# Two-layer graph transformer, 1024 nodes: a chunk of the output projection between the last two transpositions, and earlier spreading of the row sums

## The reference, cut

```python
for l in range(2):                       # the two attention rounds
    q = ((x @ Wq[l].T + bq[l]) * scaling).reshape(n, 8, 64)
    k = (x @ Wk[l].T).reshape(n, 8, 64)
    v = (x @ Wv[l].T).reshape(n, 8, 64)
    scores = jnp.einsum('ehd,ehd->eh', q[tgt], k[srcidx])     # one per edge and head
    w = softmax of scores over the edges of one target
    agg = segment_sum(w[:, :, None] * v[srcidx], tgt)
    attn = agg.reshape(n, 512) @ Wo[l].T + bo[l]
    x = batchnorm(x + attn, g1[l], beta1[l])
    x = batchnorm(x + relu(x @ W1[l].T + b1[l]) @ W2[l].T + b2[l], g2[l], beta2[l])
```

## Time and profile before

| | us |
|---|---|
| median of the runs shown | 1031.21 (1028.3 to 1032.97, 3 runs) |
| the profiled execution, device time | 1029.51 |
| its span, first to last instruction | 1027.7 |
| TensorE busy | 957.7 |
| VectorE, ScalarE, GpSimd busy | 625.0, 494.3, 251.2 |
| mean granted TensorE clock | 0.98 |

### The profile page before, as it was taken

The page is one execution under the profiler, slowest core; times in us unless marked ns, Lnnn a source line. Parts: engine busy times, 40 slices in busy tenths (PEclk is TensorE's granted clock), DMA queues, the critical chain, the costliest instruction groups (busy, mean ns, idle before and its releaser), DMA issues.

```text
span 1027.7 us, 15261 instructions
## 1 busy us (share of the span) xinstructions
PE 957.7 (93%) x5378; PEld 682.8 (66%) x5378; DVE 625.0 (61%) x1087; ACT 494.3 (48%) x767; POOL 251.2 (24%) x138
## 2 busy tenths in 40 slices
PE   6999999999998999999999999999999999999925
PEld 2835545888777886877777776746777776767313
DVE  4676476468777324437776675535576767636395
ACT  1665344555724213327666675213576666641054
POOL 2000000599932051410100047112100000660400
PEclk9999999999999999999999999999999999999967
DMA  9201100000200111146565673111076556712102
GB/s 328 73 0 41 41 1 21 1 1 1 83 1 1 50 73 41 62 143 184 169 189 180 186 223 103 41 41 42 21 210 188 177 164 186 235 52 66 39 1 82
DMA packets 58848, 96.14 MB, mean 94 GB/s; under 512 B 8284, under 2 KB 38172, under 8 KB 58270
## 3 DMA queue, kind: packets, MB, share of 16 engines
q1 hardware_dynamic: 55454, 93.11, 28.8%
q10 hardware_dynamic: 3328, 2.15, 0.7%
HBM read 59.58 MB, written 33.55 MB: 91 GB/s over the span
## 4 chain that ended last, share of the span: by engine, by line
PE 74%; POOL 7%; issue 6%; DVE 6%; ACT 4%; DMA 2%; SPq 0%; DVEq 0%; ACTq 0%; POOLq 0%
PE slots L1802 66%; PE slots L1869 9%; POOL MASK L702 3%; POOL MASK L696 1%; POOL KR L701 1%; DMA W<-in_wkT 1%; POOL X L733 1%; DMA PT<-blocks 1%; POOL PT L693 1%; ACT X L1118 1%; DVE X L1686 0%; POOL WL L713 0%; DVE SM L1663 0%; DVE st L1163 0%; ACT XTR L816 0%
## 5 line engine op out<-in xcount | busy, mean ns | idle before, releaser
L1802 PE MATMUL slots<-PT,XN 128*64 128x256 f32 x1024 | 117.6, 382 | 0.4 <-DMA PT<-blocks 0.2
L1591 DVE CUSTOM_DVE_ANT_0 SM<-slots,MASK 128x1024 f32<-128x1024 f32 x64 | 75.7, 1220 | 66.2 <-PE slots L1802 66.2
L1802 PE MATMUL slots<-KS,QS 64*128 64x512 f32 x768 | 105.7, 406 | 4.6 <-DVE nm L1591 3.5
L1802 PEld LDWEIGHTS slots<-PT,XN 128*64 128x64 f32 x1024 | 72.0, 137 | 42.8 <-issue 11.7
L758 POOL TENSOR_TENSOR QS<-QF,QS 128x512 fp32r<-128x512 f32 x16 | 20.7, 1291 | 320.4 <-ACT QS L1038 320.4
L1802 PEld LDWEIGHTS slots<-KS,QS 64*128 64x128 f32 x768 | 70.3, 184 | 25.1 <-issue 10.4
L805 ACT ACTIVATE PT<-slots 128x1024 f32<-128x1024 f32 x68 | 69.4, 1020 | 31.1 <-PE slots L1869 26.2
L1022 ACT ACTIVATE SM<-SM,nm 128x1024 f32<-128x1024 f32 x64 | 73.3, 1145 | 18.8 <-DVE nm L1591 18.1
L1022 ACT ACTIVATE PT<-PT,nm 128x1024 f32<-128x1024 f32 x64 | 73.3, 1145 | 16.9 <-DVE nm L1591 16.5
L1802 PE MATMUL slots<-PT 128*128 128x512 bf16 (+3 forms) x408 | 78.8, 364 | 2.3 <-ACT PT L805 1.2
L1591 DVE CUSTOM_DVE_ANT_0 PT<-slots,MASK 128x1024 f32<-128x1024 f32 x64 | 75.2, 1211 | 4.1 <-PE slots L1802 3.9
(11 more groups left out here) (403 smaller groups left out, 2163.1 us busy)
## 6 DMA issues: line engine op xcount, KB each, us to landing
blocks<-FL SPq DMA_DIRECT2D x56, 512.0 KB, 3.2
PT<-blocks SPq DMA_DIRECT2D x224, 128.0 KB, 3.4
X<-in_x SPq DMA_DIRECT2D x4, 512.0 KB, 11.9
W<-in_wout SPq DMA_DIRECT2D x2, 1024.0 KB, 6.2
W<-in_gq SPq DMA_DIRECT2D x2, 1024.0 KB, 5.1
W<-in_gk SPq DMA_DIRECT2D x2, 1024.0 KB, 5.1
spill<-X SPq DMA_DIRECT2D x4, 512.0 KB, 2.6
SXR<-XTR SPq DMA_DIRECT2D x1, 2048.0 KB, 8.4
```

What stands on the lines that cost most here:

```text
L1591: nc.vector.tensor_tensor_reduce(out=SMs[n % SMB], in0=src, in1=MASK[:, unit(n)[2], :], scale=-1.0, scalar=-0.1 * NO_EDGE, op0=ALU.add, op ...
L1802: return nc.tensor.matmul(o_, lhsT, rhs, start=start, stop=stop)
```

## The change

Two things. In `attention_order`, `rsum_bc` stands ahead of the pair of scores of its step and no longer behind it (0 to 2 in each round; `rsum_bc` 3 has no scores beside it). And in the tail, `wo` 0 is begun before `turn` 63: its chunk 0 stands between `turn` 62 and `turn` 63, chunks 1 and 2 right behind `turn` 63, ahead of `rsum` 3. For this the slots are given by a table: one slot is skipped at `rsum` 3 of each round, so that `wo` 0 has the slot of `turn` 61; `rsum` 3 has that of `agg` 14, `agg` 15 that of `turn` 62, `rsum_bc` 3 that of `turn` 63. All later jobs follow on, each four slots behind its forerunner as before. With the moved `rsum_bc`, six jobs around each take another forerunner: at the third one, for example, score 59 has the slot of score 56, not 57.

```diff
--- before.py
+++ after.py
@@ -68,10 +68,10 @@
         m = n - LAG
         if 0 <= m < UNITS:
             order += [("flip" if i in FLIPS_BEFORE else "turn", i) for i in (m, m + 1)]
+        if m >= 16 and m % 16 == 4 or m == UNITS + 2:
+            order.append(("rsum_bc", m // 16 - 1))
         if n < UNITS:
             order += [("score", n), ("score", n + 1)]
-        if m >= 16 and m % 16 == 4 or m == UNITS + 2:
-            order.append(("rsum_bc", m // 16 - 1))
         if n % 8 == 4 and 8 <= n < UNITS - 8:
             order.append(("q", n // 8 + 1))
         if n == 4:
@@ -173,6 +173,14 @@
 
 JOBS = job_table()
 INDEX = {name: j for j, (name, _) in enumerate(JOBS)}
+SLOT, SLOT_BEFORE, _last, _at = {}, {}, [None] * 4, 0
+for _name, _ in JOBS:
+    if _name[0] in ("rsum0g", "rsum1g") and _name[1] == H // 2 - 1:
+
+        _at += 1
+    SLOT[_name], SLOT_BEFORE[_name] = _at % 4, _last[_at % 4]
+    _last[_at % 4] = _name
+    _at += 1
 EVAC_COUNT = {}
 _seen = {"act": 0, "dve": 0, "dve_xT": 0}
 for _name, _engine in JOBS:
@@ -456,7 +464,7 @@
         shift_added, out_summed, nibbles_added, hid_cleared, w1_split, sum_ready = (
             sem(n) for n in ("shift_added", "out_summed", "nibbles_added", "hid_cleared", "w1_split", "sum_coefficients_ready"))
 
-        slot_of = lambda name, i: psum[:, INDEX[(name, i)] % 4, :]
+        slot_of = lambda name, i: psum[:, SLOT[(name, i)], :]
 
         def evacuated(name, i):
             engine = JOBS[INDEX[(name, i)]][1]
@@ -1789,9 +1797,8 @@
 
             def begin(name, i):
 
-                j = INDEX[(name, i)]
-                if j >= 4:
-                    wait(*evacuated(*JOBS[j - 4][0]))
+                if SLOT_BEFORE[(name, i)]:
+                    wait(*evacuated(*SLOT_BEFORE[(name, i)]))
                 return slot_of(name, i)
 
             def need(name, *idx):
@@ -2230,17 +2237,19 @@
                         if n % 2 == 1:
                             both_heads(l, n - 1)
                     elif step == "turn":
+                        if n == UNITS - 1:
+
+                            begin(f"wo{l}", 0)
+                            project(l, 0, (0,))
                         wait(probs, UNITS * l + n + 1)
                         for s in range(TT):
                             last = turn(slot[:, s * P:(s + 1) * P], SMs[n % SMB][:, s * P:(s + 1) * P])
                         end(last)
+                        if n == UNITS - 1:
+                            project(l, 0, (1, 2))
                     elif step == "rsum":
                         wait(recips, H // 2 * l + n + 1)
                         end(turn(slot[0:16, 0:P], rl[:]))
-                        if n == H // 2 - 1:
-
-                            begin(f"wo{l}", 0)
-                            project(l, 0, (0, 1, 2))
                     elif step == "rsum_bc":
                         need(f"rsum{l}g", n)
                         wait(sel_made, 1)
```

## The result

| | before | changed |
|---|---|---|
| median, first comparison | 1031.67 (4 executions, 1028.3 to 1032.97) | 1022.06 (4 executions, 1021.11 to 1022.76) |
| profiled execution, device time (span) | 1029.51 (1027.7) | 1021.41 (1019.6) |
| mean granted clock of the profiled execution | 0.980 | 0.986 |
| same two kernels in two later comparisons | 1030.22 and 1029.39 | 1024.51 and 1024.89 |

The ratio of the first comparison is 0.9919, with an interval of 0.9896 to 0.9942; of the later two 0.9939 (0.9911 to 0.9968) and 0.9953 (0.9937 to 0.9970). So the change makes the kernel faster, by 0.5 to 0.8%; why the comparisons differ is part of what follows. One execution of before, 1631.04 us at a mean granted clock of 0.557, is in none of the numbers.

What follows compares the result with a forecast made beforehand. TensorE, busy for 93% of the span, bounds the kernel. Tails 1.6 + 1.6 and sums 0.2 make 3.4, with 0.8 of clock 4.2, off the median 1031.21: 1027.0 us, range 1023.2 to 1030.3.

Steps and rivals of the forecast that it cites:

- What bounds, and which waits go: TensorE bounds the kernel; in both tails its waits for unit 63's exponential and transposition 63's copy go, the rest moves forward.
- The size of a tail: End of each attention round, transposition 62 to `agg` 15: 1.6 us gained at full clock, about 6.75 left of 8.38.
- The cross-check: First tail: TensorE's two waits there, 0.74 and 0.86, sum to 1.60, matching the 1.6 us worked out.
- The delay of transposition 63 and of `rsum` 3: In the tail, transposition 63 starts 0.8 later and `rsum` 3 comes 3.7 later; both covered, by 2 us or more.
- The sums ahead of the scores: `rsum_bc` 0 to 2 of each round: 0.1 gained at each of two places, nothing at the other four, 0.2 in all.
- the third place: `rsum_bc` 2 of each round, before scores 58, with no projection behind the scores: 0.1 to 0.2 worked out, 0.1 taken.
- The prediction's sign: Before scores 58, TensorE's wait for the score evacuation was to stand at 0.6 to 0.7 still.
- its own start at 614.5: First round, scores 58 after the sums' move: worked out to start at 614.5 instead of 614.66.
- The clock: Second tail's nine slow matmuls: 1.6 us if the clock no longer falls; half, 0.8, taken for a typical execution.
- The rival that the clock gives more: Most executions of before fall in both tails, none of after: 3.4 + 3.2 = 6.6 gained, 1024.6; chance 0.27.
- the low end of the range: Whole kernel's median time: 1023.2 us, set by the rival with clock falls in both tails and a little.
- half a fall: Tails: one of two had the clock fall, priced 1.6 us, so 0.8 was counted as saved in a typical execution.

Runs made afterwards that it cites:

- e1: Against the changed kernel, only the accumulator's new slot kept: all chunks of `wo` 0 behind `rsum` 3, sums behind the scores; median 1026.95, ratio to before 0.9968.
- e5: Changed kernel with both tail gaps put back: TensorE waits for unit 63's exponential before chunk 0, for transposition 63's copy before chunks 1 and 2; 1029.84, ratio to before 0.9998.

## Why the prediction was right, and where not

- *What bounds, and which waits go*: right. Both waits, `ACT PT L1022` and `ACT PT L805`, are gone from both tails, nothing was late in their place, and the rest moved as a block: from `agg` 15 to the scores of the next round the distance to before stays at 1.91 to 1.93 until the clock enters. e1 shows the accumulator's part (1.05 a tail) and the chunk's (1.16).
- *The size of a tail*: the term of the sum that was too small. 1.6 was forecast, 2.2 came. I priced eight transpositions at 1.03, a distance read off where scores follow them; with the projection behind them the next matmul starts after 0.85 and 0.79 (637.80 - 636.95, 640.07 - 639.28). The 18 matmuls took 1.48 + 2.85 = 4.33, where 1.58 + 2.96 was worked out and before took 4.31; only `rsum` 3 was dearer, 0.20 for 0.10. Together 6.17 for 6.75. From start to start, before against after, the tail reads: transposition 62 to what follows 1.83 and 0.85, transposition 63 1.11 and 0.79, `rsum` 3 1.13 and 0.20, the matmuls 4.31 and 4.33. The cross-check, which summed the idle brackets to 1.60, had the same fault: a bracket counts from the end of the instruction before (636.65 + 1.09 = 637.74), but the next one could have started 0.85 after that one's start (637.50), in its shadow. So the bracket behind transposition 62 is 0.24 short of what filling it is worth, that behind `rsum` 3 0.15 (in e1 the matmul starts 0.12 after the start of `rsum` 3, which counts as 0.27 long): 2.0 for the two. The last 0.2 is that transposition 63 has another neighbour. e5 says the same from the other side: waits of 0.75 and 1.17 cost 2.44, not 1.92.
- *The delay of transposition 63 and of `rsum` 3*: covered, as worked out. ScalarE's copy of 63 (640.41 by its timeline, 1.03 long) was done 1.7 before `agg` 15.
- *The sums ahead of the scores*: 0.24 up to scores 58 at the third place, where 0.1 to 0.2 was worked out and 0.1 taken. The wait did not grow, though the scores came late by the full 0.93, because the scores that have to wait are released by score 56 and no longer by 57. The prediction's sign, a wait of still 0.6 to 0.7, failed, it is 0.39; its own start at 614.5 would have made it 0.54. What it did not look at is the step behind: `agg` 12 waits for moved blocks, and with the 0.07 at each of the other four places nothing is left of the gain on average.
- *The clock*: 0.8 was forecast for a typical execution, from one fall in two tails. The profiled execution gave its 1.6 back, as worked out for it; there 1024.5 was forecast and 1021.41 came, 0.6 more a tail, 0.3 more at the third places and the rest by falls elsewhere (699 and the last stage) that had not been counted. The rival that the clock gives more, with the falls in both tails, would have given 1024.6, and the three medians of the changed kernel lie at 1022.1, 1024.5 and 1024.9; but it is not its mechanism that did it. At an equal clock the gain is 4.9 +- 0.6, and by the rows 4.4. In the means of all executions (17 of the changed kernel, 65 of before) it is 1029.8 - 1023.8 = 6.0, and without the four of the first comparison 5.4. The 9.6 of the first comparison is 4.9 plus a set of four executions of before that were 2 us above its own long-run median and a set of four of after at a mean clock of 0.985, 0.003 above what the same kernel had later (worth 2); 0.7 is left over, and why both sets lay that way stays open. The first median, 1022.06, lies 1.1 below the low end of the range, the later two inside it. The forecast of 1027.0 was 2 to 3 us too high for the typical execution of the changed kernel. About 1.5 of it is its base: the median of three executions of before, 1031.21, where the 65 later ones have 1029.67. What was subtracted from it, 4.2, is near the 4.5 and 5.7 of the later comparisons, and that is partly luck: the tails gave 1.2 more than their 3.2, the third places nothing instead of 0.2, and that half a fall is saved, the 0.8, is not shown (0.4 +- 0.6 by the mean clocks).
- *The page*: the section "A second HAM failure mode: psum-queue depth-cycling" of the Trainium skill (TensorE: Matmul & The Clock Gate) has short gaps between groups of matmuls bring the lower clock again and again. The prediction preferred it to the rule of "Part 1: The HAM clock gate" on account of one row. The profiled executions have falls behind the two short gaps in two of six passages and in none of 14 without, which speaks for it and is too few to show it; the mean clocks of 134 executions show that such gaps are not what makes the excess of the first comparison.

## What to carry to other kernels

A step whose operands are ready early is best placed where the engine that bounds the kernel waits, and it is worth the idle time shown plus the overlap of neighbours that the wait had cut off, here 2.2 for 1.6; look which row stands behind the filled place, since the distance from one kind of instruction to the next depends on both. Where single executions scatter with the granted clock, compare kernels at an equal clock before a difference is explained: two sets of four were enough here to make 5 to 6 us look like 9.6. And a wait that vanishes in one place because a step was pulled forward (`agg` 13) can come back as three where the step's own inputs are younger (`agg` 12): follow a gain to the next step that waits for something else, here a transfer, before it is counted, and over more than one profile.

## What was not expected of the hardware

By the trace TensorE does not start its matmuls strictly in program order: in the changed kernel the first score matmul (which reads rows of one head, 64 partitions) starts at 611.60, ahead of the last two of the eight spreading matmuls (also 64 partitions) at 611.71, which stand before it in the program. The same order stands at the third place of every profile in which the sums come right ahead of the scores. A mean clock lower by 0.001 goes with 0.65 us more over the kernel, and one and the same program had means from 0.975 to 0.986 (before), with 1025.8 to 1034.4 us.
